# A graph network's edge stage: TensorE runs both halves of a unit's sums before the products and transposes of later units

## What is computed

```python
w_m = (efeat @ W_msg + b_msg).reshape(E, in_f, -1)      # 16 x 16 for each edge
w_a = (efeat @ W_attn + b_attn).reshape(E, in_f, -1)
h_src = feat[src][:, :, None]
e1 = w_m * h_src
e2 = w_a * h_src
seg_max = jax.ops.segment_max(e2, dst, num_segments=N)
ex = jnp.exp(e2 - seg_max[dst])
denom = jax.ops.segment_sum(ex, dst, num_segments=N)
attn = ex / denom[dst]
ft = jax.ops.segment_sum(e1 * attn, dst, num_segments=N)
return ft.sum(axis=1)
```

## Time and profile before

| | us |
|---|---|
| median of 3 runs | 2403.3 (2400.13 to 2404.92) |
| span of the profiled execution, first to last instruction | 2618.5 |
| of it up to 880 us, the first stage | 880.0 |
| of it the edge stage | 1738.5 |

### The profile page before, as it was taken

One profiled execution on the slowest core, in us unless ns is written; L12 is line 12 of the kernel. 1 busy time (PEld: TensorE's weight loads), 2 busy tenths in 40 slices (PEclk: granted clock), 3 DMA queues, 4 the chain that ended last, 5 costly groups with the idle time before them and its releaser, 6 DMA issues.

```text
span 2618.5 us, 37987 instructions
## 1 busy us (share of the span) xinstructions
PE 1880.0 (72%) x5814; PEld 706.3 (27%) x5815; DVE 1989.2 (76%) x3269; ACT 1458.7 (56%) x4999; POOL 1289.6 (49%) x1520
## 2 busy tenths in 40 slices
PE   2445676577982577787887777877888877888855
PEld 1111111132341133233333333333333333333322
DVE  5678999752011588888888888888898898988866
ACT  5124444210001576676777767777776776776643
POOL 2200000425556566656666657666666665666650
PEclk9789989788975699999999989999998998998877
DMA  2000000000001000000000000000000000000000
GB/s 31 17 23 4 0 0 0 2 10 17 11 13 15 9 10 10 9 10 9 10 9 10 9 10 9 10 9 10 9 10 9 10 10 9 9 10 9 9 5 7
DMA packets 85243, 25.74 MB, mean 10 GB/s; under 512 B 61677, under 2 KB 82271, under 8 KB 85087
## 3 DMA queue, kind: packets, MB, share of 16 engines
q0 software_dynamic: 36672, 18.09, 5.7%
q1 hardware_dynamic: 48463, 6.91, 1.8%
q10 hardware_dynamic: 80, 0.43, 0.1%
HBM read 22.73 MB, written 2.51 MB: 10 GB/s over the span
## 4 chain that ended last, share of the span: by engine, by line
issue 29%; DVE 25%; PE 23%; DVEq 17%; ACT 3%; POOL 1%; another core or an unknown queue 1%; DMA 1%; ACTq 0%; POOLq 0%; PEldq 0%; PEld 0%
PE pair L820 9%; DVE eo L1471 6%; DVE hot L1197 4%; DVEq L1490 4%; PE pw L711 3%; DVE eo L1514 2%; DVE eo L1505 2%; PE pw L807 2%; PE pw L708 2%; PE pw L707 2%; DVE top L1486 2%; ACT eo L1021 2%; DVE top L1491 2%; DVE bank L1499 2%; DVEq L1503 1%
## 5 line engine op out<-in xcount | busy, mean ns | idle before, releaser
L626 POOL DMA_INDIRECT nbr<-table,rec x928 | 961.0, 1036 | 527.3 <-ACT eo L1021 274.0
L820 PE MATMUL pair<-eo,ident 128*128 128x512 f32 x1856 | 890.0, 625 | 12.4 <-issue 7.7
L1021 ACT ACTIVATE eo<-pw,nbr 128x32 f32<-128x32 f32 x3712 | 694.3, 371 | 83.1 <-issue 66.9
L1471 DVE TENSOR_TENSOR eo<-pw,nbr 128x1024 f32 (+1 forms) x348 | 412.5, 1218 | 169.3 <-PE pw L807 94.4
L820 PEld LDWEIGHTS pair<-eo,ident 128*128 128x128 f32 x1856 | 366.2, 201 | 494.9 <-issue 479.6
L807 PE MATMUL pw<-wk,termsT 100*128 100x512 bf16 x928 | 307.5, 417 | 249.8 <-issue 173.8
L1197 DVE TENSOR_SCALAR hot<-iota_key,near_key 128x500 bf16<-128x500 f16 x974 | 273.8, 346 | 59.3 <-issue 31.9
L1010 ACT ACTIVATE eo<-eo 128x2048 f32<-128x2048 f32 x116 | 221.5, 1910 | 107.4 <-DVE eo L1505 85.1
L1514 DVE TENSOR_TENSOR eo<-eo x232 | 272.7, 1216 | 5.9 <-issue 4.0
L1505 DVE TENSOR_TENSOR eo<-eo,bank (+1 forms) x116 | 265.3, 2287 | 10.7
L672 PE MATMUL bank<-hot 128*128 128x500 bf16 x488 | 146.7, 414 | 145.4 <-DVE hot L1197 93.1
(11 more groups left out here) (245 smaller groups left out, 1815.6 us busy)
## 6 DMA issues: line engine op xcount, KB each, us to landing
nbr<-table,rec POOLq DMA_INDIRECT x928
rec<-unit_recs SPq DMA_DIRECT2D x116, 8.0 KB
attr<-in_edge_attr_dram,rec POOLq DMA_INDIRECT x116
unit_recs<-place SPq DMA_DIRECT2D x27, 64.0 KB
shared<-key_row SPq DMA_DIRECT2D x1, 1600.0 KB, 6.7
counts<-in_dst_dram SPq DMA_DIRECT2D x1, 448.0 KB
counts<-in_src_dram SPq DMA_DIRECT2D x1, 448.0 KB
place<-in_src_dram,at_i POOLq DMA_INDIRECT x26, 2.6
```

Source lines behind the costliest of these rows:

```text
L626: pool.indirect_dma_start(nbr[:, b, j * FEAT:(j + 1) * FEAT], None, table, bass.IndirectOffsetOnAxis(ap=rec[:, b, j:j + 1], axis=0)).then_ ...
L820: mm = pe.matmul(total, ident[:], eo[:, ring, j * 2 * CH:(j + 1) * 2 * CH], start=False, stop=(j == SLOT - 1), skip_group_check=True)
L1021: done = act.activation(eo[:, ring, lo:lo + wide], pw[:, j - 4, c * wide:(c + 1) * wide], ACT.Copy, scale=nbr[:, held, j * FEAT + c:j * FE ...
L1471: dve.tensor_tensor(eo[:, bass.ds(ring, 1), k * 4 * CH:(k + 1) * 4 * CH] .rearrange("p r (c f) -> p (r c) f", f=2 * FEAT), pw[:, 2 * (k % ...
```

## The change

In `pe_unit`, the second half of the sums moves ahead of product 1 of unit u + 3. All else keeps its place.

```diff
                 sums(b % RING, 0, u)
+                sums(b % RING, 1, u)
                 if ahead > 2:
                     product((b + 3) % 2, 1, u + 3)
-                sums(b % RING, 1, u)
                 if ahead > 3:
                     turn(b % 2, 0, u + LEAD)
```

## The result

| | before | changed |
|---|---|---|
| measured, median us | 2401.7 (2391.4 to 2404.9, 4 runs) | 2418.1 (2416.4 to 2420.9, 4 runs) |
| span of the profile shown | 2618.5 | 2415.8 |

The changed kernel takes 1.0092 times as long, with an interval of 1.0073 to 1.0111. The two medians of the table alone give 1.0068, and three later sessions gave 1.0067 to 1.0077, so the loss is some 16 to 20 us. It is slower, and the forecast was faster.

What follows compares the result with a forecast made beforehand. The prediction took DVE in the edge stage to be the bound, waiting for PE's product 2 behind a blocked product 1. Its terms, -17 + 4 = -13 us, led from 2403.3 us to 2390 us, range 2335 to 2412 us.

Steps and rivals of the forecast that it cites:

- the 113.6 us: DVE's idle time ahead of L1471 in the profile before, the most the change could win in the profiled execution.
- the 215 us: Gap between the profile's span of 2618.5 us and the timed 2403.3 us, 8.2%, suspected to be the cost of recording.
- from the profile to the clock: Step from span to timed runs: recording makes the holes, so most of the 113.6 us is probably not in 2403.3 us.
- -17 + 4 = -13 us: Whole-kernel sum: 17 us of DVE waits won, 4 us lost in units after tile ends, giving 2390 us.
- 15% of 113.6 us left to win, 17 us: Share of DVE's recorded waits ahead of L1471 taken as really present in the timed runs and removable.
- the room of 0.6 us: Time between product 1's end and DVE's need of it in the new order, if the sums begin on time.
- the closed hole: PE's 2.14 us wait ahead of product 1, which the change closes; this was to speak for fewer slow halves.
- the term of 4 us: Loss in 22 units after tile ends, about 0.2 us each, because their sums begin late; bounds 0 and 17 us.
- rival 3: Slower: PE's clock falls between sums in ordinary units, late product 1 makes DVE wait; 35 us, 2408 to 2430 us, chance 0.18.
- L1471 as one block of three: Sign in ordinary units: DVE's three pieces run without a wait between them and the unit lasts 12.7 us.
- some 2509 us: Sign: the profile's span after the change, from 2618.5 - 113.6 + 4, falling much more than the measured time.
- 2335: Lower end of the range in us, if two thirds of the recorded waits are real; 0.08 lies below.

Runs made afterwards that it cites:

- e16: Kernel before with two copies of 512 columns added on ACT ahead of last_pair's 32 activations, on a chip without holes: 2481.4 us, ratio 1.0347.
- e10: Kernel before with two copies of 512 columns added on ACT ahead of last_pair's activations, on a chip with holes: 2764.1 us, ratio 1.0245.
- e11: Changed kernel with two copies of 512 columns added ahead of last_pair's activations, on a chip with holes: 2666.1 us, ratio 0.9832 to the kernel before.
- e12: Changed kernel with two needless matmuls between product 1 and the first transpose, chip with holes: 2663.0 us, ratio 0.9869 to the kernel before.
- e4: Kernel before with product 1 moved to the middle of the second half of the sums, chip with holes: 2644.8 us, ratio 0.9743.
- e2: Changed kernel with every transpose issued twice, chip with holes: 2754.7 us, ratio 1.0131 to the kernel before.
- e13: The kernel before, unchanged, profiled on a chip without holes: 2398 us.
- e14: The changed kernel, unchanged, on a chip without holes: 2414.9 us, ratio 1.0077 to the kernel before.
- e7: Changed kernel with product 3 issued twice, chip without holes: 2414.3 us, ratio 1.0076 to the kernel before.
- the split order: Kernel before with product 1 in the middle of the second half of the sums: ratios 1.0006 and 1.0003 without holes, 0.9743 with holes.
- e1: The kernel before, unchanged, profiled on a chip with holes: 2709 us.
- e3: Kernel before with every transpose issued twice, chip with holes: 3280.6 us, ratio 1.2079.

## Why the prediction was wrong

**The reading of the queue was right, where there are holes.** Product 1 waits for last_pair and holds up the second half of the sums, and DVE pays at the third piece; e16 shows it by itself (8.2 us become 88.5), e10 and e11 show that the new order pays far less of it (193.3 and 47.9 us). How much of the 113.6 us could have been won on such a chip was not measured, since the changed kernel never ran on one. Of four kernels that have product 1 later and something else changed, three took 1.3 to 2.6% less than the kernel before there (e12, e11, e4) and one 1.3% more (e2).

**What the 215 us were.** The step "from the profile to the clock" took the difference between span and median for the cost of recording. In every later session the span agreed with the time, with holes and without, and e13 was recorded and has no holes. So the 215 us are most likely the difference between two chips, or between two sessions, and not the cost of recording alone. The conclusion that most of the 113.6 us is not in the 2403.3 us came out right all the same, by luck, since its reason was wrong: it is 8.2 us. The Trainium skill, NOTIFIC — the notification-queue block, section 7.1 Overflow: three behaviours, one of which stalls the engine, was drawn on for it. These runs neither bear it out nor refute it: what makes the holes, and whether recording has a part in them on the chips that have them, is open.

**The steps that failed.** Two steps of the sum -17 + 4 = -13 us. The first is the term "15% of 113.6 us left to win, 17 us". There were 11.5 us of waits before, 8.0 of them after tile ends, where none of the three orders tried has less (8.0, 8.8 and 10.2 us); in ordinary units 2.6 us could be won. The second, which turned the sign, is a loss in ordinary units that the sum put at nothing: it let the sums begin on time there, so that the room of 0.6 us would do, because the closed hole was to keep the clock up. In e14 the sums begin late in 15 of the 61 ordinary units, and these units wait 11.5 us. By kind of unit, e14 against e13, the change cost 9.1 us in ordinary units, 2.2 after tile ends and 3.9 at tile ends, 15.2 us together. So the term of 4 us for the units after tile ends measured 2.2, and the 3.9 us at the tile ends themselves were not in the prediction.

**The rival that was right.** The main loss is rival 3, with its mechanism, its place and its mark (a wait of DVE after the first of its three pieces) as it was put: the clock falls in ordinary units, the sums begin late, and the room of 0.6 us is used up. It was given 0.18 and 2408 to 2430 us; 2418 lies in its middle. Its count was 44 units of 0.8 us each, 35 us; measured are 15 of 61, of 0.7 to 0.85 us each. What was argued against it, that the closed hole would keep the clock up, looked at the wrong stretch. It closed the hole within the sums and left the part after the sums as thin, only longer, 4.5 us in place of 2.9. And without holes in ACT's work the gap ahead of product 1 was 0.93 us and the clock did not fall in any ordinary unit of e13, so there was nothing to give back. The Trainium skill, TensorE: Matmul & The Clock Gate, section Part 1: The HAM clock gate, has it that activity releases the throttle. That agrees with e7, where more work in the thin part left no fall in ordinary units, but it had to be asked of every stretch of the new order and not of the one that the change closes.

**The range and the marks.** The profile after was to show L1471 as one block of three; it does in most units, and the wait after the first piece that "would be rival 3" is there. Its other mark, a clock below the 0.92 of the earlier trace rows, is not met by the number: it is 0.93, but 0.96 is what the kernel before has without holes. The idle time ahead of L1471 is 21.8 us, not under 20. The span was to be some 2509 us; that compared across chips and says nothing. Two readings were off without an effect on the forecast: two thirds of 113.6 us less 4 us lead to 2332 us, not 2335, and during PE's wait of 2.59 us in the earlier trace rows the granted clock was still 1.00; it fell as the wait ended.

## What to carry to other kernels

Before a profile's waits are priced, its span has to be held against the timed runs of the same session; where they are 9% apart, as here, the trace may be of another chip than the times, and the largest wait in it may be missing from them. An operation that the next engine waits for belongs early, but not so early that its own wait blocks ready work: half way, as in the split order, cost nothing where there was no hole (1.0003 and 1.0006) and won 2.6% where there was. And when dense work is gathered into one block, look at what is left outside it: in this kernel that thinner part decided at which clock the next block began.

## What the runs showed of the hardware

- The same program takes 2704 and 2722 us on two chips and 2396 and 2397 us on three others, one session each. Where it is long, ACT pauses in the middle of a run of 32 independent activations: 191 pauses without a releaser from 900 to 2700 us in e1, 126.7 us together, and none in e13. The first stage is longer there too (the first unit's L1514 stands at 894 us in e1 and at 839 in e13).
- On such a chip eight small matmuls more in each unit cost 21% (e3), in another order of the same work 1.3% (e2). In e3 ACT's cast of the transposes waits, about once a unit, for something that the profile does not name: 110 times from 900 to 3260 us, 714.5 us together.
- PE's clock fell in ordinary units after a part in which PE's pieces were short and apart, without a wait of over 0.62 us: over the 105 units the changed kernel has 43 stretches and 201 us of 1.4 ms at the lower level, the kernel before 21 and 99 us, and with product 3 doubled it is 22 stretches in the changed order and 17 in the old one.
